# Routing's matmuls ahead of the linear layer's products within a step of TensorE

## The chip, the cores and the metric

The kernel runs on one core of a Trainium2 chip. A core has TensorE (matrix products, results in PSUM), VectorE, ScalarE and GpSimd, each with a list of its own that it works through in order, and SyncE, which starts DMAs. The lists are tied together by semaphores: an instruction waits until a count is reached. The metric is the time on the device in microseconds; lower is better.

## The reference, cut to what matters

Four layers over x, 2048 tokens of 512 floats (8 x 256 x 512), each with a layer norm ahead and x added behind. The change touches the first two.

```python
x = x + attn0(layernorm(x))     # data @ (blockwise masked weight).T + bias
x = x + ffn0(layernorm(x))      # routing, below
x = x + attn1(layernorm(x))     # latent K/V attention, 32 heads
x = x + ffn1(layernorm(x))      # gated feed forward, 1376 wide

# ffn0
logits = flat @ router_weight.T + router_bias       # 64 experts
scores = softmax(logits)
topk_w, topk_idx = top_k(scores, 8)
out = flat * topk_w.sum(-1) + w_dense @ expert_bias  # w_dense: topk_w at topk_idx
```

## The kernel before

The first stages run over 16 tiles of 128 tokens in a software pipeline. `head_steps` makes the steps s = 0 to 30; in step s the linear layer (`SparseLinear`) works on tiles near s and routing (`RoutedBias`) on tiles near i = s - 6. Each engine has its own loop over the steps and takes the linear layer's part, then routing's, then K/V tasks (`now`), which exist only from step 23 on. There is no planner; the order within a step is the order in the code.

TensorE's part of a step, with the letters used below (line numbers are those of the profile's rows):

- F, `flip`, L714: four transposes that turn linear's h of tile s - 2 into a bank of PSUM (steps up to 17).
- P, the products, L738: twelve matmuls of 512 columns for tile s - 3 (three passes over high and low parts, four chunks), in steps 3 to 18. P waits for the low part of the turned tile (`lo_done`) from VectorE, and gives `y_done`.
- C, L937: one transpose of the chosen experts' weights, tile i - 4, from step 10 on.
- N, L945: four transposes of the next layer's h, tile i - 9, from step 15 on.
- M, L952: the mix, one product with the experts' bias, tile i - 5, from step 11 on.
- L, L959: the logits, four small products, tile i - 2, from step 8 on.
- T, L967: four transposes of routing's h, tile i - 1, from step 7 on. T and C write the same bank of PSUM (`ps_c = ps_t`), so each waits until ScalarE has copied out the result of the other (`await_turn_bank`).

The order before is F, P, C, N, M, L, T. At i = 0, which is step 6, TensorE also waits for routing's constants (`await_constants`), behind F and P of that step. Their last writer is GpSimd, with two memsets (L825, L827) in its own step 6. GpSimd's part of step 6 waits for other tiles' results, not for P of step 6.

ScalarE's part of a step is: the high part of F's turned tile (L67, h_hi), linear's h of the next tile (L121), exp of the logits (L860), the scaling of x (L865, needs r_combined from GpSimd), the copy of C's result (L870, r_chosen_t), the high part of N's result, routing's h (L121), the copy of T's result (L885, h1t) and the high part of one piece of K/V weights (kv_w_hi).

VectorE's part begins with the addition of P's result of the step before to x (L695, waits for `y_done`), then the statistics of x for the next layer norm (L94, L98), the low part of the turned tile (L72), and routing's top 8 and additions. GpSimd's part begins with the bias addition (L632), then the layer norm's factors (L102, L106, L108; the first L102 waits for VectorE's statistics mv_ln), routing's next h (L116), r_combined (L849, L852) and the low part of a piece of K/V weights (L72, kv_w_lo, which waits for kv_w_hi).

In the texts P(6) is P of step 6, F(10) is F of step 10, and so on.

Of the kernel before, what the change touches and what calls it, by code (L numbers as in the profile page):

```python
# [530 lines left out]
class SparseLinear:  # L531
# [190 lines left out]
        pe.matmul(self.ps_b, self.same_block[:, :], self.row_sums[:, :], start=True, stop=True).then_inc(self.blocks_done, 1)  # L722
        self.flip(pe, 1)

    def pe_body(self, pe, i):
        if 2 <= i - 2 < TILES:
            self.flip(pe, i - 2)
        if 0 <= i - 3 < TILES:
            t = i - 3
            pe.wait_ge(self.lo_done, t + 1)  # L730
            if t >= 2:
                pe.wait_ge(self.x_done, t - 1)
            tokens = self.tokens(t)
            for c in range(KC):
                if t == 0:
                    pe.wait_ge(self.w_lo_done, c + 1)
                for n, (a, b) in enumerate(PASSES):
                    last = pe.matmul(self.ps_y[:, t % 2, :], tokens[a][:, c, :], self.w0[b][:, c, :],  # L738
                                     start=(c == 0 and n == 0), stop=(c == KC - 1 and n == 2))
            last.then_inc(self.y_done, 1)  # L740
# [257 lines left out]
def first_stages(nc, sem, sb, ps, split, x, ident, half, consts, ln, weights, h3, kv_w, query, operands, sources, router_sources, kv_weights, wq_g, k_scr, v_scr):  # L998
# [14 lines left out]
    with ExitStack() as st:  # L1013
# [8 lines left out]
        with ExitStack() as shared:  # L1022
            linear = SparseLinear(sem, sb, split, bank, x, ident, half, consts, ln[0], ln[1], h3, sources, shared)
# [19 lines left out]
        def freed(eng, n):  # L1043

            before = [m for m in range(n) if bank_of[m] == bank_of[n]]
            if not before:
                if bank_of[n] >= 4:
                    eng.wait_ge(routed.lo_done, TILES)
                else:
                    eng.wait_ge(linear.lo_done, TILES)  # L1050
                    eng.wait_ge(linear.x_done, TILES)
            elif before[-1] in down_count:
                eng.wait_ge(z_done, down_count[before[-1]])
            elif before[-1] in stage_count:
                eng.wait_ge(staged, stage_count[before[-1]] + 1)
            else:
                eng.wait_ge(lo_done, lo_count[before[-1]])

        def outlet(n):

            _, _, a, b = tasks[n]
            return ([p[:, a, :, 4 * b:4 * b + 4, :].rearrange("p b h m -> p h b m") for p in latent],
                    bank[:, bank_of[n], :].rearrange("p (h b m) -> p h b m", h=4, b=4))
# [28 lines left out]
        with nc.Block() as block:  # L1092
            @block.gpsimd
            def _(pool):
                linear.pool_start(pool)
                for s, i, p, _ in steps:
                    if s >= 2:
                        linear.pool_body(pool, s)
                    if i == 0:
                        routed.set_constants(pool, linear)  # L1100
                    routed.pool_body(pool, i)
                    if 0 <= p < KV_PIECES:
                        piece_lo_part(pool, p)
                query.make(pool, 0)
# [80 lines left out]
            @block.vector  # L1185
            def _(dve):
                def task(n):
                    if n in lo_count:
                        dve.wait_ge(hi_done, lo_count[n])
                        parts, src = outlet(n)  # L1190
                        lo_part(dve, parts, src).then_inc(lo_done, 1)
                    if n in given_at:
                        query.given_lo_part(dve, given_at[n], 0)
                    if n in step_lo_at:
                        operands.step_lo(dve, step_lo_at[n])
                    if n in step_at:
                        if step_at[n] == 0:
                            dve.wait_ge(routed.lo_done, TILES)
                            dve.wait_ge(piece_lo, KV_PIECES)
                        operands.step_sum(dve, step_at[n])  # L1200

                linear.dve_start(dve)
                for s, i, _, now in steps:
                    if s >= 2:
                        linear.dve_body(dve, s)
                    if i == 0:
                        routed.await_constants(dve)
                    routed.dve_body(dve, i)
                    for n in now:
                        task(n)  # L1210
                for n in range(paired, len(tasks)):
                    task(n)

            @block.tensor
            def _(pe):
                awaited = set()

                def task(n):
                    kind, quad, a, b = tasks[n]
                    if kind in pieces_of and kind not in awaited:  # L1220
                        awaited.add(kind)
                        pe.wait_ge(piece_lo, pieces_of[kind])
                    freed(pe, n)
                    out = bank[:, bank_of[n], :]
                    if kind == "Z":
                        pe.wait_ge(routed.lo_done, (quad + 1) * TILES // 2)
                        for c in range(KC):
                            for m, (u, v) in enumerate(PASSES):
                                tokens = h3[u][:, c, quad * SPAN:(quad + 1) * SPAN].rearrange("p (n j) -> p n j", j=8)[:, :, a]
                                last = pe.matmul(out, tokens, down_w[v][:, c, :], start=(c == 0 and m == 0), stop=(c == KC - 1 and m == 2))  # L1230
                    elif kind == "C":
                        pe.wait_ge(z_done, down_count[at[("Z", quad, 2 * a + 1, 0)]])
                        for h in range(4):
                            last = pe.transpose(out[:, h * P:(h + 1) * P], z[:, a % 2, 4 * b + h, :, :].rearrange("p j l -> p (j l)"), ident[:, :])
                    elif kind == "K":
                        if (a, b) == (0, 0):
                            pe.wait_ge(lo_done, lo_count[at[("C", quad, 1, 1)]])
                        for c in range(2):
                            for m, (u, v) in enumerate(PASSES):
                                last = pe.matmul(out, up_w[0][u][:, c, b * HEAD:(b + 1) * HEAD],  # L1240
                                                 latent[v][:, c, 2 * a:2 * a + 2, :, :].rearrange("p b h m -> p (b h m)"),
                                                 start=(c == 0 and m == 0), stop=(c == 1 and m == 2))
                    else:
                        if (a, b) == (0, 0):
                            pe.wait_ge(lo_done, lo_count[at[("C", quad, 3, 1)]])
                        for c in range(2):
                            for m, (u, v) in enumerate(PASSES):
                                rows = latent[u][:, 2 + c, a // 2, 4 * (a % 2):4 * (a % 2) + 4, :].rearrange("p h m -> p (h m)")
                                last = pe.matmul(out, rows, up_w[1][v][:, c, b * HID:(b + 1) * HID],
                                                 start=(c == 0 and m == 0), stop=(c == 1 and m == 2))  # L1250
                    last.then_inc(task_done, 1)

                linear.pe_start(pe)
                for s, i, _, now in steps:
                    if s >= 3:
                        linear.pe_body(pe, s)
                    if i == 0:
                        routed.await_constants(pe)
                        pe.wait_ge(linear.on_done, 1)
                    routed.pe_body(pe, i)  # L1260
                    for n in now:
                        task(n)
                for n in range(paired, len(tasks)):
                    task(n)
# [1155 lines left out]
```

## Time and profile before

| what | us |
|---|---|
| median of 3 runs | 1679.67 (1678.84 to 1681.83) |
| the profiled execution, its own time | 1679.91 |
| its span, first to last instruction | 1678.0 |
| TensorE busy | 1631.0 |
| VectorE, ScalarE, GpSimd busy | 1164.2, 924.4, 843.8 |
| mean granted clock of TensorE | 0.997 |

The span is the profile's own clock, from the first instruction to the last; the execution's time has 1.91 us more around it. Rows of a timeline give the start, the duration, the engine, the line of the kernel, the operation and the tiles out<-in; a bracket gives the engine's idle time just before and what released it. "L738" there is a line of the kernel, while L alone is the letter for the logits. Matmuls overlap, so the distance from one start to the next says how long one holds the engine, not its duration.

### The profile page before, as it was taken

To read this page: it belongs to the slowest core of one execution; us is meant where nothing else is said; L and a number is where in the kernel's file an instruction comes from. 1 tells how busy PE (TensorE), PEld (TensorE's weight loads), DVE (VectorE), ACT (ScalarE), POOL (GpSimd) and SP (SyncE) were. 2 spreads that over 40 slices of the span, in tenths; PEclk is the share of its full clock that TensorE was granted. 3 is DMA by queue.
4 is the path that set the end of the run, shared out by engine and by line. 5 is a ranking of instruction groups with operands and counts; after the bars stand their busy time and mean duration, and the time that the engine had idled before them with its cause. 6 is when DMAs were issued, how large, how long until landed. Compare 5 with 4: busy or idle time off the path is not lost. (4 is left out here: it accounts for less than half of the span.)

```text
span 1678.0 us, 26468 instructions
## 1 busy us (share of the span) xinstructions
PE 1631.0 (97%) x8298; PEld 1370.3 (82%) x8298; DVE 1164.2 (69%) x2990; ACT 924.4 (55%) x2464; POOL 843.8 (50%) x1257
## 2 busy tenths in 40 slices
PE   6989999999999999999999999999999899999999
PEld 4868887788888888888888888888888788877887
DVE  6883254776776776667667767767767588787776
ACT  3764455665765665666566556657657443434432
POOL 4883003634634644544445346446446297708752
PEclk9999999999999999999999999999999999999999
DMA  5011754111111111134111111111110021113111
GB/s 170 26 29 60 274 178 145 51 63 38 51 64 38 41 51 54 46 101 163 64 40 50 63 39 51 63 39 51 64 38 26 32 76 63 39 32 113 51 51 50
DMA packets 62489, 114.98 MB, mean 69 GB/s; under 512 B 5584, under 2 KB 25040, under 8 KB 58256
## 3 DMA queue, kind: packets, MB, share of 16 engines
q1 hardware_dynamic: 62352, 113.30, 20.4%
q8 instruction: 68, 1.11, 0.3%
q14 instruction: 69, 0.57, 0.1%
HBM read 84.97 MB, written 28.31 MB: 68 GB/s over the span
## 5 line engine op out<-in xcount | busy, mean ns | idle before, releaser
L1854 PE MATMUL ps_q<-kv_w_hi,o_hi 128*128 128x512 f32 x512 | 203.5, 397 | 4.5 <-DVE o_lo L72 4.5
L1854 PE MATMUL ps_q<-kv_w_lo,o_hi 128*128 128x512 f32 x512 | 200.0, 391 | 0.0
L1854 PE MATMUL ps_q<-kv_w_hi,o_lo 128*128 128x512 f32 x512 | 199.7, 390 | 0.0
L72 POOL TENSOR_TENSOR kv_w_lo<-w_raw,kv_w_hi 128x512 fp32r<-128x512 f32 x128 | 163.1, 1291 | 57.3 <-ACT kv_w_hi L67 57.3
L1796 PE MATMUL ps_q<-h_hi,kv_w_hi 128*128 128x512 f32 x448 | 181.9, 406 | 3.0 <-PEq L1092 1.5
L1796 PE MATMUL ps_q<-h_lo,kv_w_hi 128*128 128x512 f32 x448 | 175.4, 392 | 0.0
L1796 PE MATMUL ps_q<-h_hi,kv_w_lo 128*128 128x512 f32 x448 | 175.0, 391 | 0.0
L67 ACT ACTIVATE kv_w_hi<-w_raw 128x512 fp32r<-128x512 f32 (+1 forms) x240 | 126.6, 566 | 64.1 <-POOL w_raw L260 62.8
L1383 POOL TENSOR_SCALAR prob<-prob,inv_sum 128x128 f32<-128x128 f32 x256 | 95.3, 372 | 103.6 <-DVE inv_sum L1601 103.3
L67 ACT ACTIVATE o_hi<-ps_o 128x512 fp32r<-128x512 f32 x128 | 76.3, 596 | 127.2 <-PE ps_o L1836 127.1
L1439 ACT ACTIVATE prob<-prob,neg_max 128x128 f32<-128x128 f32 x256 | 100.2, 392 | 83.0 <-DVE neg_max L1596 83.0
L255 POOL TENSOR_TENSOR w_raw<-w_raw 128x512 f32<-128x512 f32 x16 | 26.4, 1648 | 220.1 <-DVE kv_w_lo L72 220.1
L1626 DVE TENSOR_TENSOR x<-ps_q,x 128x512 f32<-128x512 f32 x128 | 87.8, 686 | 67.7 <-PE ps_q L1854 67.7
L72 POOL TENSOR_TENSOR h_lo<-v_raw,h_hi 128x512 fp32r<-128x512 f32 x32 | 41.1, 1283 | 184.8 <-ACT h_hi L67 184.8
L1441 ACT ACTIVATE prob<-prob,neg_max 128x256 f32<-128x256 f32 x256 | 126.8, 495 | 0.0
L72 DVE TENSOR_TENSOR o_lo<-ps_o,o_hi 128x512 fp32r<-128x512 f32 x128 | 88.0, 688 | 51.3 <-ACT o_hi L67 51.2
L1384 POOL TENSOR_SCALAR prob<-prob,inv_sum 128x256 f32<-128x256 f32 x256 | 122.7, 479 | 0.0
L1594 DVE CUSTOM_DVE_ANT_0 prob<-ps_s,causal 128x128 f32<-128x128 f32 x256 | 74.3, 290 | 66.0 <-PE ps_s L1812 64.8
L1854 PEld LDWEIGHTS ps_q<-kv_w_hi,o_hi 128*128 128x128 f32 x512 | 96.2, 188 | 28.5 <-issue 10.4
L1854 PEld LDWEIGHTS ps_q<-kv_w_lo,o_hi 128*128 128x128 f32 x512 | 96.1, 188 | 20.5
L2329 PE MATMUL f_ps_r<-h_hi,kv_w_hi 128*128 128x512 f32 x280 | 109.5, 391 | 2.1 <-DVE f_part_U L2203 1.9
L1854 PEld LDWEIGHTS ps_q<-kv_w_hi,o_lo 128*128 128x128 f32 x512 | 96.3, 188 | 18.3
(236 smaller groups left out, 4868.1 us busy)
## 6 DMA issues: line engine op xcount, KB each, us to landing
w_raw<-in_wq_g SPq DMA_DIRECT2D x16, 1024.0 KB, 4.8
w_raw<-in_wo_g SPq DMA_DIRECT2D x16, 1024.0 KB, 4.7
k_raw<-k_scratch SPq DMA_DIRECT2D x32, 256.0 KB, 3.4
v_raw<-v_scratch SPq DMA_DIRECT2D x32, 256.0 KB, 3.8
f_gate_raw<-in_gate_c SPq DMA_DIRECT2D x10, 512.0 KB, 4.9
f_up_raw<-in_up_c SPq DMA_DIRECT2D x10, 512.0 KB, 3.6
f_down_raw<-in_down_c SPq DMA_DIRECT2D x10, 512.0 KB, 4.0
x<-in_x SPq DMA_DIRECT2D x16, 256.0 KB, 2.8
```

What stands on the lines that cost most here:

```text
L67: return act.activation(parts[HI], src, ACT.Copy)
L72: return dve.tensor_tensor(parts[LO], src, parts[HI].bitcast(F32), ALU.subtract)
L255: pool.tensor_tensor(self.block("S1"), self.block("A21"), self.block("A22"), ALU.add).then_inc(self.made, 1)
L1383: pool.tensor_scalar(prob[:, b, h, 0:P], prob[:, b, h, 0:P], inv_sum[:, b, h, 0:1], 1.0, ALU.mult, ALU.mult)
L1384: pool.tensor_scalar(prob[:, b, h, P:3 * P], prob[:, b, h, P:3 * P], inv_sum[:, b, h, 1:2], 1.0, ALU.mult, ALU.mult).then_inc(normed, 1)
L1439: act.activation(prob[:, b, h, 0:P], prob[:, b, h, 0:P], ACT.Exp, scale=-1.0, bias=neg_max[:, b, h, 0:1], accum_out=row_sum[:, b, h, 0:1])
L1441: act.activation(prob[:, b, h, P:3 * P], prob[:, b, h, P:3 * P], ACT.Exp, scale=-1.0, bias=neg_max[:, b, h, 1:2], accum_out=row_sum[:, b, ...
L1594: dve.tensor_tensor_reduce(out=prob[:, b, h, 0:P], in0=ps_s[:, h, 0:P], in1=causal[:, P:2 * P], scale=-SCALE, scalar=3.0e38, op0=ALU.add, ...
L1626: dve.tensor_tensor(x[:, t, :], ps_q[:, half, :], x[:, t, :], ALU.add).then_inc(y_read, 1)
L1796: done = pe.matmul(ps_q[:, i, :], left[s][:, c, i * HEAD:(i + 1) * HEAD], right[t][:, c, :], start=(c == 0 and m == 0), stop=(c == 1 and m ...
L1854: done = pe.matmul(ps_q[:, half, :], o[b][i][:, half, h, :], wo[j][:, h, :], start=(h == 0 and m == 0), stop=(h == GROUP - 1 and m == 2))
L2329: last = pe.matmul(bank(kind, k, name), stationary[a], feed.operand(right)[b][:, c, :], start=(c == 0 and m == 0), stop=(c == 1 and m == 2))
```

## The change

`pe_body` of the linear layer is cut in two: `pe_flips` holds F, `pe_products` holds P. TensorE's loop calls the first where `pe_body` was and the second behind routing's part. The order of a step becomes F, C, N, M, L, T, P, and in step 6 P also comes behind the wait for the constants. The other engines' lists, all instructions and all DMAs are the same.

```diff
-    def pe_body(self, pe, i):
+    def pe_flips(self, pe, i):
         if 2 <= i - 2 < TILES:
             self.flip(pe, i - 2)
+
+    def pe_products(self, pe, i):
         if 0 <= i - 3 < TILES:
             t = i - 3
             pe.wait_ge(self.lo_done, t + 1)
@@
                 for s, i, _, now in steps:
                     if s >= 3:
-                        linear.pe_body(pe, s)
+                        linear.pe_flips(pe, s)
                     if i == 0:
                         routed.await_constants(pe)
                         pe.wait_ge(linear.on_done, 1)
                     routed.pe_body(pe, i)
+                    if s >= 3:
+                        linear.pe_products(pe, s)
                     for n in now:
                         task(n)
```

## Rows read from the trace of the kernel before

**Rows 1.** The page: busy time of each engine over the span.
```profile
PE 1631.0 (97%) x8298; PEld 1370.3 (82%) x8298; DVE 1164.2 (69%) x2990; ACT 924.4 (55%) x2464; POOL 843.8 (50%) x1257
```

**Rows 2.** Windows: length; busy PE, PEld, DVE, ACT, POOL; granted clock; DMA share, GB/s.
```profile
34.40:37.80 3.40, 3.34 (x10) 2.86 (x11) 2.78 (x7) 2.00 (x3) 2.39 (x6) 0.52 0.00 0
...
106.00:109.50 3.50, 3.33 (x11) 2.33 (x11) 2.80 (x11) 2.07 (x8) 2.97 (x9) 0.53 0.02 5
...
121.50:185.00 63.50, 63.09 (x296) 56.18 (x296) 20.81 (x42) 29.44 (x59) 15.54 (x31) 1.00 0.27 97
```

**Rows 3.** Waits from 29 to 122 us: in total, times, longest.
```profile
ACT x L865 <- POOL r_combined L852: 12.4, 8, 2.7
...
PE kv_banks L937 <- ACT h1t L885: 4.7, 5, 1.0
...
POOL kv_w_lo L72 <- ACT kv_w_hi L67: 2.6, 2, 2.3
```

**Rows 4.** Timeline of TensorE, steps 6 to 18: start, duration, what.
```profile
28.86 0.60 PE L714 MATMUL kv_banks<-ident,h 128*128 128x128 f32 x4
...
34.46 1.11 PE L714 MATMUL kv_banks<-ident,h 128*128 128x128 f32 x4 [2.25 <-POOL r_chosen L827]
...
44.23 0.60 PE L714 MATMUL kv_banks<-ident,h 128*128 128x128 f32 x4
...
47.43 1.00 PE L959 MATMUL kv_banks<-router,h1t 128*128 128x64 f32 x8
...
52.02 1.00 PE L959 MATMUL kv_banks<-router,h1t 128*128 128x64 f32 x8
52.86 0.61 PE L967 MATMUL kv_banks<-ident,h 128*128 128x128 f32 x4
53.30 0.60 PE L714 MATMUL kv_banks<-ident,h 128*128 128x128 f32 x4
...
80.99 0.63 PE L967 MATMUL kv_banks<-ident,h 128*128 128x128 f32 x4 [0.30 <-ACT r_chosen_t L870]
...
94.17 0.48 PE L738 MATMUL kv_banks<-w_hi,h_hi 128*128 128x512 f32 x1
...
97.00 0.27 PE L937 MATMUL kv_banks<-ident,r_chosen 128*128 128x128 f32 x1
...
98.41 1.00 PE L959 MATMUL kv_banks<-router,h1t 128*128 128x64 f32 x8
```

**Rows 5.** Timeline of ScalarE, steps 6, 11 and 15.
```profile
29.50 0.60 ACT L67 ACTIVATE h_hi<-kv_banks 128x512 fp32r<-128x512 f32 x1 [1.90 <-PE kv_banks L714]
...
54.30 0.59 ACT L67 ACTIVATE h_hi<-kv_banks 128x512 fp32r<-128x512 f32 x1
54.78 0.81 ACT L121 ACTIVATE h<-x,factors_ln 128x512 f32<-128x512 f32 x1
55.48 0.34 ACT L860 ACTIVATE r_exp<-logits,r_neg_max 128x64 f32<-128x64 f32 x1
...
79.87 0.81 ACT L865 ACTIVATE x<-x,r_combined 128x512 f32<-128x512 f32 x1 [1.50 <-POOL r_combined L852]
80.59 0.26 ACT L870 ACTIVATE r_chosen_t<-kv_banks 128x128 f32<-128x128 f32 x1
```

**Rows 6.** Timeline of VectorE, steps 8, 14, 15 and 19; GpSimd's last.
```profile
39.51 0.69 DVE L695 TENSOR_TENSOR x<-kv_banks,x 128x512 f32<-128x512 f32 x1 [2.25 <-PE kv_banks L738]
...
70.25 0.68 DVE L695 TENSOR_TENSOR x<-kv_banks,x 128x512 f32<-128x512 f32 x1
...
75.97 0.68 DVE L695 TENSOR_TENSOR x<-kv_banks,x 128x512 f32<-128x512 f32 x1
...
100.90 0.68 DVE L695 TENSOR_TENSOR x<-kv_banks,x 128x512 f32<-128x512 f32 x1
...
102.28 0.18 DVE L98 BATCH_NORM_AGGREGATE mv_ln<-bn_ln 128x2 f32<-128x6 f32 x1
...
104.12 0.21 POOL L102 TENSOR_SCALAR ve_ln<-mv_ln 128x1 f32<-128x1 f32 x1
```

## The prediction

> **What bounds the kernel now.** I read the page first: TensorE is busy for 97% of the span [rows 1]. That is an average, so the second view is the windows over the stage that the change touches (steps 6 to 18 of the first stages, about 29 to 104 us). It shows where TensorE is not full: at 34.4 us it comes back from a wait at half clock (0.52), and at 106 us again (0.53); from 121.5 us on it is busy for 63.09 of 63.50 us [rows 2]. So two things count: when the first K/V product starts (121.5 us), because behind it TensorE alone sets the pace, and what sets that start.
>
> The list of waits for 29 to 122 us says what does: ScalarE waits 12.4 us in 8 places for GpSimd's r_combined [rows 3]. GpSimd is the slow engine of the steady state, and TensorE and ScalarE stand by for it. In TensorE's own timeline the steps 8 to 13 have no gap at all, and from step 15 on T waits for the copy of the turned choice (80.99, 0.30 idle) [rows 4]. GpSimd needs from TensorE, above all, the statistics of x behind each P: VectorE adds the product to x, takes the statistics, and GpSimd's first piece for that tile (L102) starts right behind them. At 39.51 VectorE itself waited 2.25 us for a P [rows 6]. Therefore the question is when the P of each step ends, up to the last one in step 18.
>
> **What the change moves.** No instruction is added or taken away, no DMA moves, and no queue but TensorE's changes. In each of the steps 6 to 18 the twelve matmuls of P go behind C, N, M, L and T. In steps 3 to 5 nothing of routing exists, so nothing moves. Three costs follow.
>
> *1. Step 6.* There is nothing of routing in it but the wait for the constants, and that wait now stands ahead of P(6), the products of tile 3, which used to run from 29.2 us. GpSimd's memset releases it at 34.46 us [rows 4], and its own work doesn't depend on P(6). So P(6) starts at 34.46. The engine then works at half clock, 0.52 for 3.40 us [rows 2], which costs 3.40 x 0.48 = 1.63 us against full clock. P alone is 97.00 - 94.17 = 2.83 us. P(6) ends at 34.46 + 2.83 + 1.63 = 38.9. Step 7 is then F and P (47.43 - 44.23 = 3.20) and T (0.44, from 52.86 to 53.30): F(8) at 42.6. Steps 8 and 9 are F and P, L (52.86 - 52.02 = 0.84) and T, 4.48 us each, as before: F(9) at 47.0, F(10) at 51.5, where it was at 44.23 + 4.48 = 48.7 [rows 4]. TensorE is 2.8 us late.
>
> *2. Steps 10 to 17.* From step 10 on T overwrites the bank of C, so it waits until ScalarE has copied C's result out. Before, P stood between F and T and hid that wait. Now F (0.37), C, N and M (1.41) and L (0.84) stand ahead of T, 2.6 us at most, and P stands behind T. ScalarE's list of the step starts with the copy of F's result, so each step is one closed chain: F start to copy 29.50 - 28.86 = 0.64; copy to h 0.48; h to exp 0.70; exp 0.34 [rows 4, 5]; scale to chosen copy 80.59 - 79.87 = 0.72 [rows 5]; that copy to T 80.99 - 80.59 = 0.40; T 0.44; P 2.83; and then the next F. Sum 6.55 us. Seven steps (10 to 16) give F(17) at 51.5 + 45.9 = 97.4, where TensorE's own work was only 4.6 to 5.9 us a step. In step 17 the h of linear's next tile is gone (0.70 less): 103.2. Step 18 has no F, and TensorE's work fills it: C, N, M 98.41 - 97.00 = 1.41, L 52.86 - 52.02 = 0.84, T 0.44, P 2.83 [rows 4], together 5.5: P(18) ends at 108.8. VectorE's add of it starts 0.2 later at 109.0, where it was at 100.90; its aggregate ends 102.28 + 0.18 - 100.90 = 1.56 us behind that and GpSimd's L102 follows, at 110.6, where it was at 104.12 [rows 6]. So GpSimd is 6.5 us late. In the list of waits GpSimd has only early ones [rows 3], so there is no idle time from here to step 22 to give back, and behind 121.5 us TensorE is full [rows 2], so 6.5 us reach the end. That the late start and the loop are not added in full (P(18) is 11.8 us late, GpSimd 6.5) is because VectorE used to take P(18) 3.9 us after its end.
>
> The sum hangs on 8 handoffs. The row has 80.99 - 80.85 = 0.14 us from the end of ScalarE's copy to T [rows 4, 5]. The Trainium skill (Runtime: NRT & Kernel Launch, the section on the preamble) gives 44 ns for a semaphore's hop between engines in a barrier; with that figure, as an estimate, 8 x 0.10 = 0.8 us less, so 5.7. No run here shows a barrier's hop in this place, and the sum keeps the trace's 0.14.
>
> *3. The clock.* In step 10 TensorE has F, C and L, about 1.3 us, but not yet N and M; T can start 0.64 + 0.48 + 0.70 + 0.34 + 0.72 + 0.40 = 3.28 us behind F, so it waits 2.0 us. The trace before has no such wait in this place. Nearest row: 2.25 us of idle before 34.46 and the clock is at half behind it [rows 2, 4]; from the other side: of five waits of up to 1.0 us for ScalarE's h1t, from 100 us on, one was followed by half clock, the others by full [rows 2, 3]. 2.0 us is nearest to the first. So I take one fall, for its price of 1.63 us; it lies on the closed chain (T and P of step 10) and goes to the end in full. The bounds are 0 and, with a second fall in a later step (each has 1.1 us of idle), 3.3.
>
> What costs nothing: C, N, M and L now run earlier, hidden under ScalarE's part of the chain; if ScalarE were quicker they would cost up to 2.6 us a step. VectorE's list of a step is 75.97 - 70.25 = 5.7 us long [rows 6], under the 6.55. In step 7 GpSimd's kv_w_lo waited 2.3 us for a copy behind T [rows 3]; T is now ahead of P(7), but P(6) is ahead of T, which starts at 38.9 + 0.4 = 39.3, so I book no gain (rival D has it).
>
> Sum: 6.5 + 1.6 = 8.1 us. The profiled execution's own time, 1679.91, gives 1688.0; it lies 0.24 above the median of the runs, 1679.67, which gives 1687.8 (+0.49%).
>
> **Rivals.**
> A, the clock stays up in step 10: for it, that 1.0 us waits mostly passed; against it, the length of the wait. 6.5 us, 1686.2. Chance 0.18.
> B, the clock falls again in steps 11 to 22: the waits of 1.1 us a step are new, and at 106 us it fell once in such a stretch, hidden by GpSimd then [rows 2, 3]. 8.1 + 1.6 to 3.3, about 1690.3. Chance 0.12.
> C, the other side, not slower: T's wait for ScalarE's copy stays covered, because the copy of F and the four activations get done while C, N, M and L run. Then a step lasts as long as TensorE's work (4.6 to 5.9 us), GpSimd sets the pace again from step 10, and at most the 2.8 us of point 1 are left: by a little less, 2.6 us, 1682.3, within the noise. It decides if ScalarE's part is under 2.6 us; the rows give 3.3. Chance 0.08.
> D, gain: the turn ahead of P gives ScalarE and GpSimd their work sooner, and GpSimd's 2.6 us of waits for kv_w_hi go [rows 3]. For it: GpSimd is the bound. It holds only if P(6) is done by the time VectorE was through with step 7, 39.51 - 2.25 = 37.3 [rows 6], against 38.9. 1677.1. Chance 0.05, half of it with more gain than the noise.
> My forecast has 0.57; its own range, with a chain of 6.3 to 6.8 us a step (0.25 either way, seven times), is 1686.5 to 1690.
>
> **How the numbers follow.** 0.2% is 3.4 us, about what a measurement of this kernel can tell from no change. Slower by more than that: forecast, A and B, 0.87. Within: C and half of D, 0.10. Faster: 0.03. The range has to take in A and the lower part of B, and reach towards C: 1683.5 to 1691.0 leaves out D, most of C and the upper part of B, under 2 in 10.
>
> **What the new profile would show.** TensorE idle about 5 us up to 34.46, then twelve L738-type matmuls first; VectorE's add of step 7 at 39.0 instead of 34.44. In each of the steps 10 to 17 T (the turn) with idle before it, released by ScalarE's r_chosen_t, 2.0 us in step 10 and 1.1 us after; F to F 6.55 us. A window of half clock from about 55 us. The last P ending near 110 us, GpSimd's waits for mv_ln appearing in steps 11 to 13 and 19, and the first K/V product at 128 to 130 us; everything behind it shifted and otherwise the same. The prediction is wrong if F to F stays at 5.5 us (C), if no window but 34.4 and one late one is at half clock (A), or if the K/V tasks win back time behind 130 us.

## The result, and the profile after

| | before | after |
|---|---|---|
| median (lowest to highest, runs) | 1679.95 (1678.84 to 1681.83, 4) | 1690.38 (1689.56 to 1693.94, 4) |
| profiled execution, its own time | 1679.91 | 1689.57 |
| its span | 1678.0 | 1687.6 |
| TensorE busy, mean granted clock | 1631.0, 0.997 | 1635.0, 0.994 |

The ratio is 1.0063 with an interval of [1.0052, 1.0075]: the change costs 0.63%, 10.5 us (8.7 to 12.6). The forecast was 1687.8, 8.1 us more; the range, 1683.5 to 1691.0, holds the median. One execution in this study, among the 12 of e7 below, took 2340.83 us at a mean granted clock of 0.655, and the comparisons leave it out. The kernel with the change has other line numbers: F is L714, P L740, C L939, N L947, M L954, L L961, T L969, GpSimd's last memset L829, ScalarE's copy of C L872, its copy of T L887.

The page's row of busy time. Against [rows 1] the averages say next to nothing: the same instructions, TensorE 4 us busier.

```profile
PE 1635.0 (97%) x8298; PEld 1374.3 (81%) x8298; DVE 1164.1 (69%) x2990; ACT 925.0 (55%) x2464; POOL 843.9 (50%) x1257
```

The waits from 29 to 135 us (total, times, longest) say where it went.

```profile
ACT h_hi L67 <- PE kv_banks L714: 28.4, 11, 9.1
DVE x L695 <- PE kv_banks L740: 19.4, 12, 8.2
POOL ve_ln L102 <- DVE mv_ln L98: 12.0, 7, 6.5
...
PE kv_banks L969 <- ACT r_chosen_t L872: 6.1, 7, 1.7
...
PE kv_banks L740 <- POOL r_chosen L829: 5.0, 1, 5.0
...
POOL kv_w_lo L72 <- ACT kv_w_hi L67: 0.8, 3, 0.3
```

In [rows 3] GpSimd was the engine that the others waited for: ScalarE stood by for r_combined, 12.4 us. That row is gone. Now GpSimd itself waits, 12.0 us (6.5 of them in step 7), for statistics that VectorE takes behind P, VectorE waits 19.4 us for P, ScalarE 28.4 us for F, and TensorE 6.1 us for ScalarE's copy of C. Each engine waits for the next one in a ring. GpSimd's wait for kv_w_hi fell from 2.6 to 0.8 us, but an engine that waits 12 us elsewhere gains nothing from that.

TensorE's timeline of step 6 and the start of step 7 (start, duration; a bracket is idle time before and what released it), to be read against [rows 4]:

```profile
27.28 0.60 PE L714 MATMUL kv_banks<-ident,h 128*128 128x128 f32 x4
32.84 0.80 PE L740 MATMUL kv_banks<-w_hi,h_hi 128*128 128x512 f32 x1 [4.96 <-POOL r_chosen L829]
...
38.12 1.02 PE L714 MATMUL kv_banks<-ident,h 128*128 128x128 f32 x4
```

And of steps 10 and 11, where T now stands ahead of P:

```profile
51.13 0.60 PE L714 MATMUL kv_banks<-ident,h 128*128 128x128 f32 x4
51.56 0.27 PE L939 MATMUL kv_banks<-ident,r_chosen 128*128 128x128 f32 x1
51.67 1.00 PE L961 MATMUL kv_banks<-router,h1t 128*128 128x64 f32 x8
54.40 0.63 PE L969 MATMUL kv_banks<-ident,h 128*128 128x128 f32 x4 [1.73 <-ACT r_chosen_t L872]
54.78 0.48 PE L740 MATMUL kv_banks<-w_hi,h_hi 128*128 128x512 f32 x1
...
57.63 0.60 PE L714 MATMUL kv_banks<-ident,h 128*128 128x128 f32 x4
...
60.90 0.63 PE L969 MATMUL kv_banks<-ident,h 128*128 128x128 f32 x4 [0.87 <-ACT r_chosen_t L872]
...
64.11 0.60 PE L714 MATMUL kv_banks<-ident,h 128*128 128x128 f32 x4
```

F to F is 6.50 and 6.48 us, with TensorE idle before each T. ScalarE's timeline of step 10 shows what T waits for: five activations back to back behind F, and the copy of C is the fifth.

```profile
51.76 0.60 ACT L67 ACTIVATE h_hi<-kv_banks 128x512 fp32r<-128x512 f32 x1 [1.34 <-PE kv_banks L714]
52.26 0.80 ACT L121 ACTIVATE h<-x,factors_ln 128x512 f32<-128x512 f32 x1
52.96 0.34 ACT L862 ACTIVATE r_exp<-logits,r_neg_max 128x64 f32<-128x64 f32 x1
...
53.29 0.81 ACT L867 ACTIVATE x<-x,r_combined 128x512 f32<-128x512 f32 x1
54.00 0.26 ACT L872 ACTIVATE r_chosen_t<-kv_banks 128x128 f32<-128x128 f32 x1
```

The windows (length; busy PE, PEld, DVE, ACT, POOL; granted clock; DMA share, GB/s) for the stretches behind a wait, for the start of K/V, and for three stretches far behind it:

```profile
32.80:38.60 5.80, 5.76 (x15) 4.51 (x16) 0.07 (x1) 0.00 (x0) 1.27 (x1) 0.50 0.00 0
51.10:57.60 6.50, 4.77 (x30) 4.11 (x29) 3.87 (x15) 4.10 (x9) 5.95 (x13) 1.00 0.06 20
113.00:119.00 6.00, 4.57 (x20) 3.35 (x20) 4.92 (x17) 3.42 (x9) 4.95 (x14) 0.72 0.10 27
128.40:192.00 63.60, 63.19 (x298) 56.24 (x298) 20.84 (x42) 29.50 (x59) 15.56 (x31) 1.00 0.26 97
285.00:315.00 30.00, 27.28 (x143) 22.78 (x141) 21.25 (x68) 19.95 (x62) 14.01 (x22) 0.94 0.25 81
1305.00:1335.00 30.00, 25.48 (x123) 20.40 (x122) 19.59 (x37) 9.81 (x18) 2.59 (x2) 0.94 0.11 35
1515.00:1545.00 30.00, 28.92 (x128) 24.01 (x129) 20.35 (x30) 13.84 (x31) 20.73 (x28) 0.94 0.42 140
```

The same three late stretches of the kernel before:

```profile
285.00:315.00 30.00, 26.95 (x146) 21.90 (x144) 23.69 (x71) 21.01 (x63) 15.07 (x23) 1.00 0.26 88
1305.00:1335.00 30.00, 26.96 (x138) 21.82 (x137) 17.88 (x34) 12.20 (x22) 4.11 (x5) 1.00 0.13 45
1515.00:1545.00 30.00, 28.70 (x125) 22.85 (x124) 20.91 (x29) 14.45 (x34) 25.98 (x32) 1.00 0.36 123
```

**Reading times from a common start.** The release, the end of GpSimd's last memset in step 6, fell at 34.41 us in the profile before and at 32.78 in the one after. The change doesn't set it. The kernel before had one more fall of the clock, from 20 to 24 us (the windows of before and after, in this order):

```profile
20.00:24.00 4.00, 3.15 (x10) 2.67 (x11) 2.11 (x5) 2.09 (x3) 3.44 (x5) 0.61 0.64 182
20.00:24.00 4.00, 3.18 (x16) 2.71 (x17) 2.09 (x5) 2.11 (x3) 3.80 (x6) 1.00 0.55 190
```

GpSimd's L102 of step 5, which waits for VectorE's statistics, then started at 27.93 us for 26.32. In eleven of the fourteen profiles of this study the release lies between 32.78 and 32.95; e11, at 34.52, has the same early fall (0.62), and e1 is at 33.35 without it. So stages are compared in time behind the release. "Tail" is the span behind the first K/V product.

| us behind the release | before | after | later by |
|---|---|---|---|
| F(10) | 14.30 | 18.35 | 4.05 |
| F(17) | 53.91 | 63.77 | 9.86 |
| VectorE's add of P(18) | 66.49 | 75.63 | 9.14 |
| GpSimd's first L102 of step 19, the one in [rows 6] | 69.71 | 77.30 | 7.6 |
| first K/V product | 87.12 | 95.69 | 8.57 |
| tail | 1556.5 | 1559.1 | 2.7 |

The span grew by 9.6 us: the release came 1.6 earlier, the stage up to K/V took 8.57 more, the tail 2.7 more. The tail has the same work (63.19 of 63.60 us busy here, 63.09 of 63.50 in [rows 2]), but the granted clock is 0.94 in three stretches of 30 us where it was 1.00. That is 0.06 x 30 = 1.8 us of lost clock each, not all of it on the path.

### The profile page after: what moved, and what is told of

Same layout as the page of the kernel before. It is cut to its first block and busy times, and to the rows that moved or that the text cites. A ratio compares the mean times of both kernels' runs of the same rounds, so it can differ in the third digit from the quotient of the medians.

```text
span 1687.6 us, 26468 instructions
## 1 busy us (share of the span) xinstructions
PE 1635.0 (97%) x8298; PEld 1374.3 (81%) x8298; DVE 1164.1 (69%) x2990; ACT 925.0 (55%) x2464; POOL 843.9 (50%) x1257
## 5 line engine op out<-in xcount | busy, mean ns | idle before, releaser
L255 POOL TENSOR_TENSOR w_raw<-w_raw 128x512 f32<-128x512 f32 x16 | 26.4, 1648 | 219.4 <-DVE kv_w_lo L72 219.4
L2333 PE MATMUL f_ps_r<-h_hi,kv_w_hi 128*128 128x512 f32 x280 | 109.5, 391 | 2.0 <-DVE f_part_U L2207 1.8
```

Of the source, the lines that this page charges most:

```text
L2333: last = pe.matmul(bank(kind, k, name), stationary[a], feed.operand(right)[b][:, c, :], start=(c == 0 and m == 0), stop=(c == 1 and m == 2))
```

## The experiments

Each of the twelve is compared with runs of the kernel before on the same chip. The medians of the kernel before range from 1679.95 to 1681.23 us over the chips, so an expected time can be off by about 1 us for that alone. The columns: ratio to before with its interval; then, from one profile each, the time from release to F(10) and to the first K/V product, and the tail.

| kernel | ratio | F(10) | K/V | tail |
|---|---|---|---|---|
| before | 1 | 14.30 | 87.12 | 1556.5 |
| after | 1.0063 [1.0052, 1.0075] | 18.35 | 95.69 | 1559.1 |
| a2_again | 1.0055 [1.0042, 1.0068] | 17.36 | 97.60 | 1558.2 |
| e1_p6_first | 1.0031 [1.0018, 1.0043] | 14.27 | 93.18 | 1559.3 |
| e2_only_step6 | 1.0021 [1.0012, 1.0029] | 17.74 | 91.19 | 1559.5 |
| e3_t_last | 1.0036 [1.0024, 1.0048] | 19.28 | 94.27 | 1558.3 |
| e7_warm | 1.0032 [1.0022, 1.0042] | 15.94 | 93.92 | 1558.7 |
| e5_act_order | 1.0033 [1.0020, 1.0046] | 17.24 | 91.23 | 1561.7 |
| e6_shift | 1.0039 [1.0025, 1.0053] | 14.28 | 87.14 | 1566.6 |
| e8_variance | 0.9984 [0.9975, 0.9994] | 12.67 | 82.19 | 1558.7 |
| e11_late_wait | 0.9986 [0.9977, 0.9995] | 10.26 | 83.51 | 1558.1 |
| e12_late_var | 0.9955 [0.9943, 0.9968] | 10.23 | 80.78 | 1558.7 |
| e14_after_both | 0.9997 [0.9988, 1.0006] | 10.22 | 87.22 | 1561.3 |
| e15_all | 0.9986 [0.9977, 0.9995] | 10.20 | 87.04 | 1557.9 |

**The two parts of the change, apart.** In e1 P(6) runs ahead of the wait for the constants, as before, and the other steps are as changed. In e2 only P(6) is moved behind the wait.

```diff
# e1_p6_first
                     if i == 0:
+                        linear.pe_products(pe, s)
                         routed.await_constants(pe)
...
-                    if s >= 3:
+                    if s >= 3 and i != 0:
                         linear.pe_products(pe, s)
# e2_only_step6
                         linear.pe_flips(pe, s)
+                    if s >= 3 and i != 0:
+                        linear.pe_products(pe, s)
                     if i == 0:
                         routed.await_constants(pe)
                         pe.wait_ge(linear.on_done, 1)
+                        linear.pe_products(pe, s)
                     routed.pe_body(pe, i)
-                    if s >= 3:
-                        linear.pe_products(pe, s)
```

> The change in all steps but step 6, where P(6) stays ahead of the wait for the constants. Theory (two costs: the wait in step 6, and the closed chain through T in steps 10 to 17): in the changed kernel's trace F(10) is 4.0 us late against the release of the constants, so that part goes and the chain stays, F to F 6.5 us in steps 10 to 16, and P(18) ends some 8 us later than before; GpSimd's first piece of step 19 is late by 3.6 us instead of 7.6. Time 4.0 us under the changed kernel, about 1686 (1684 to 1687). Rival, the step 6 wait is nearly all of it: 1680 to 1682. Rival, the chain is all of it: 1690.

> The order of before in all steps but step 6, where P(6) stands behind the wait for the constants. Theory: F(10) 4 us late, then TensorE's own work (4.6 to 5.9 us a step) runs without the chain and GpSimd, which is slower from step 12 on, hides part of it: 3 us over before, about 1683 (1681.5 to 1684.5). Rival, the step 6 wait is nearly all of the loss: 1688 to 1690. Rival, GpSimd hides all of it: 1680.

e1 cost 5.2 us (3.0 to 7.2), e2 3.5 us (2.0 to 4.9); their medians, 1687.25 and 1684.84, lie 0.3 us over the upper ends of the expected ranges. Their sum, 8.7, is near the change's 10.5 and a2's 9.2, so both parts are real and add up. K/V says the same: it is 6.06 us late in e1 and 4.07 in e2, and e1's profile has a fall of the clock in step 10, worth 1.6 us (below), that after's hasn't; 6.06 + 4.07 - 1.6 = 8.5 for 8.57. In e1 F(10) is where it was before (14.27), and from there every step is the closed chain. In e2 F(10) is 3.44 us late, the add of P(18) 3.39 (69.88 for 66.49) and K/V 4.07: F to F is 5.44 to 5.45 in steps 11 to 14, as before, and nothing of the late start is won back on the way, where I had expected GpSimd to hide part of it. (The 0.7 us from 3.39 to 4.07 come with a fall of the clock, 0.51 from 112.8 to 116.2 us.)

**T behind P.** F, C, N, M, L, P, T: if only T's wait ahead of P costs, moving T back should leave little more than e2.

```diff
                     if s >= 3:
                         linear.pe_products(pe, s)
+                    routed.pe_turn(pe, i)      # T, cut out of routed.pe_body
```

> The changed kernel with T behind P instead of ahead of it: F, C, N, M, L, P, T. P(6) still stands behind the wait for the constants. Theory: the chain F, ScalarE's copies, T, P is open again, since P no longer waits for ScalarE; F to F is TensorE's own 4.6 to 5.9 us in steps 10 to 14, and what is left is step 6's part: 3 to 4 us over before, about 1683.5 (1682 to 1685). Rival, it is not T's wait but P's late place in the step (VectorE's add comes late) that costs: 1688 to 1690.

It cost 6.0 us (1687.34 for the expected 1682 to 1685), and so the expectation failed. TensorE's timeline of steps 13 and 14 of e3 (P's rows left out, which run from 72.32 to 75.19):

```profile
69.51 0.60 PE L714 MATMUL kv_banks<-ident,h 128*128 128x128 f32 x4
70.45 0.30 PE L939 MATMUL kv_banks<-ident,r_chosen 128*128 128x128 f32 x1 [0.34 <-ACT h1t L887]
...
75.19 0.60 PE L971 MATMUL kv_banks<-ident,h 128*128 128x128 f32 x4
75.62 0.60 PE L714 MATMUL kv_banks<-ident,h 128*128 128x128 f32 x4
```

T no longer waits, but the bank is shared both ways: only F is left between T and the next C, where the order before has F and P, and C waits for ScalarE's copy of T. F to F is 6.11 us, and P still ends late in the step. How much of the 6.0 us is that late place and how much the wait, e3 alone doesn't tell; e14 below has P late without the closed chain and stands level with before.

**ScalarE's list.** If F to F is a chain through ScalarE, then taking F's copy and linear's h from ahead of the exp, the scaling and the copy of C should cut it, with TensorE's order as changed.

```diff
                 for s, i, p, now in steps:
+                    routed.act_chosen(act, i)   # L862, L867, L872, cut out of routed.act_body
                     if s >= 3:
                         linear.act_body(act, s)
```

> The changed kernel's TensorE order, with ScalarE's exp, scaling of x and copy of C taken ahead of linear's copy of F and h in each step. Nothing else differs. Theory: the chain of steps 10 to 17 is F, ScalarE's copy of F, h, exp, scaling, copy of C, T, P, F; with F's copy behind the copy of C it is cut, T waits no more and F to F is TensorE's own 5.45 us in steps 11 to 14. What is left is step 6 and the late P: 1684 to 1686, 4 to 6 us under the changed kernel. Rival, another wait takes its place (T or C for h1t, as with T behind P): F to F about 6 us, 1687. Rival, T's wait was not the cost: 1690.

TensorE's timeline of one step of e5:

```profile
60.85 0.60 PE L714 MATMUL kv_banks<-ident,h 128*128 128x128 f32 x4
...
63.09 0.61 PE L971 MATMUL kv_banks<-ident,h 128*128 128x128 f32 x4
...
66.29 0.60 PE L714 MATMUL kv_banks<-ident,h 128*128 128x128 f32 x4
```

T has no idle time before it, and F to F is 5.44 us in steps 11 to 13, TensorE's own work, where it was 6.50. For these steps that shows that the loop was this chain. In steps 14 to 16 F to F is 6.66 to 6.85 us: T waits again (1.01 and 0.78 us in steps 14 and 15), with ScalarE waiting for VectorE's r_neg_max and GpSimd's r_combined. The order before isn't at 5.45 there either (6.36 and 6.87 in steps 15 and 16), and over all of F(10) to F(17) the chain's loss is in steps 10 to 14: 32.5 us in after for 26.4 in before, and 13.0 for 13.2 in the two steps behind.

K/V comes 4.5 us sooner than in after (91.23 for 95.69). 1.1 us of that lies ahead of F(10), and 0.9 is the fall of the clock at 114 us that after has and e5 hasn't (see "From 6.5 to 8.57"). From F(10) to K/V before takes 72.8 us, e5 74.0 and after, less that fall, 76.4, so e5 takes away two thirds of what the chain costs there. By the ratios e5 is 5.5 us over before, where the change is 10.5, or 9.2 on e5's own chip (a2); e5's tail is 2.6 us longer than after's.

**Is the price of step 6 the clock?** e7 is the changed kernel with 52 small transposes into an unused bank ahead of the wait, so that TensorE is not idle in it.

```diff
                     if i == 0:
+                        for _ in range(52):
+                            pe.transpose(bank[:, 7, 0:P], ident[:, :], ident[:, :])
                         routed.await_constants(pe)
```

> The changed kernel with 52 extra transposes of the identity into an unused bank between F(6) and the wait for the constants, so that TensorE isn't idle there (they are no part of the computation). Theory: the half clock from 32.8 to about 38.6 us in the changed kernel's trace comes from that idle time and costs 5.8 x 0.5 = 2.9 us on the chain; it goes: 1687.5 (1686.5 to 1688.5), with F(10) about 2.9 us earlier against the release. Rival, the half clock comes anyway or GpSimd hides it: 1690 or above.

Windows of e7: behind the release, and step 10.

```profile
32.90:36.00 3.10, 3.10 (x18) 2.64 (x17) 0.00 (x0) 0.00 (x0) 1.28 (x1) 1.00 0.00 0
48.80:57.00 8.20, 6.47 (x32) 5.38 (x31) 3.84 (x15) 4.10 (x9) 7.01 (x14) 0.79 0.11 32
```

The clock is at 1.00 where it was at 0.50. From the start of P(6) to F(8) e7 takes 6.47 us and after 9.36, so the half clock costs 2.89 us. F(10) comes only 2.4 us sooner behind the release, since the transposes ran past it: P(6) starts 0.52 us behind the release in e7 and 0.06 in after. The second window shows the clock falling in step 10, which after's own profile doesn't have (1.00 from 51.1 to 57.6), so part went back. In sum e7 cost 5.4 us over before.

**The change once more,** for the clock in step 10:

> The changed kernel once more, for a second profile and a comparison of its own on the chip of the next three. Theory: the stretch from the release of the constants to the first K/V product is 95.7 us again (87.1 before), while the falls of the clock lie elsewhere from profile to profile: 1687 to 1692, and a fall in step 10 (F to F 8.1 us instead of 6.5) is seen in some profiles, as in the two experiments before, and not in others.

TensorE's timeline of step 10 and the window over it, in a2:

```profile
50.21 0.60 PE L714 MATMUL kv_banks<-ident,h 128*128 128x128 f32 x4
...
53.48 0.63 PE L969 MATMUL kv_banks<-ident,h 128*128 128x128 f32 x4 [1.73 <-ACT r_chosen_t L872]
...
54.26 0.63 PE L740 MATMUL kv_banks<-w_hi,h_lo 128*128 128x512 f32 x1
...
58.30 0.60 PE L714 MATMUL kv_banks<-ident,h 128*128 128x128 f32 x4
```

```profile
50.20:58.30 8.10, 6.37 (x31) 5.25 (x30) 3.84 (x15) 4.10 (x9) 7.03 (x15) 0.79 0.12 32
```

Same kernel, same wait of 1.73 us, and now the clock falls behind it: products of 0.63 us for 0.39, F to F 8.09 for 6.50, so 1.6 us. Of the five profiles with a wait of 1.73 us or more in step 10 four have the fall (a2, e1, e7, e14), after has not. In e5 the wait is 0.53 us and the clock stays up.

Of the expectation the clock came true and the stretch did not: K/V stands at 97.60 us and not at 95.7. F(10) is 1.0 us sooner than in after, step 10 takes 1.6 us more, and behind P(18) a2 is at half clock for twice as long as after, 21.36 us from the add of P(18) to K/V for 20.06:

```profile
115.50:122.40 6.90, 6.12 (x23) 4.40 (x21) 4.50 (x21) 4.77 (x12) 5.68 (x13) 0.51 0.15 39
```

**Does a shift ahead of K/V reach the end?** e6 is the kernel before, with 70 transposes behind the first K/V task.

```diff
                     for n in now:
                         task(n)
+                        if n == 0:
+                            for _ in range(70):
+                                pe.transpose(bank[:, 3, 0:P], ident[:, :], ident[:, :])
```

> The kernel before, with 70 extra transposes of the identity into an unused bank behind the first K/V product group (they are no part of the computation), some 6.5 to 7.5 us of TensorE time. Theory: from the first K/V product TensorE alone sets the pace, so the whole of it reaches the end: 1687 to 1688, plus 0 to 3 us where the clock falls lie otherwise than in the kernel before. Rival, later stages have slack that takes it up: under 1684.

The filler's row in e6's timeline:

```profile
123.11 7.80 PE L1265 MATMUL kv_banks<-ident 128*128 128x128 f32 x70
```

7.8 us put in, 6.5 us (4.2 to 8.9) at the end, 8.6 us in the profiled span. Within the interval all of it arrives. Up to K/V e6 is the kernel before a second time: 87.14 us for 87.12. And yet before has the fall at 106 us [rows 2] and e6 is at 1.00 from 104 to 112 us: in the order before, where GpSimd is the late engine, that fall costs nothing.

**Toward a better kernel.** Two ideas from the same reading, on the order before. e8 takes L102 from GpSimd, the engine that sets the pace, to VectorE, in both layer norms that stand there: from step 12 on that is two instructions a step. e11 takes TensorE's and VectorE's wait for the constants from step 6 to step 8, where the first logits need them. e12 has both.

```diff
# e8_variance: out of GpSimd's loop, into VectorE's; linear's part, then routing's
-            self.ln_next.variance(pool, i - 5)
+            self.ln_next.variance(dve, i - 5)
...
-            self.ln_next.variance(pool, t)
+            self.ln_next.variance(dve, t)
# e11_late_wait: in VectorE's loop, and in TensorE's
-                    if i == 0:
+                    if i == 2:
                         routed.await_constants(dve)
...
                     if i == 0:
-                        routed.await_constants(pe)
                         pe.wait_ge(linear.on_done, 1)
+                    if i == 2:
+                        routed.await_constants(pe)
```

> The kernel before with the epsilon addition of the two next layer norms (L102) on VectorE instead of GpSimd. Theory: GpSimd bounds steps 12 to 20 of the kernel before; it gives up 0.31 us in 12 steps and another 0.31 in 8, and VectorE has 0.2 us for each: the first K/V product comes 3 to 5 us earlier against the release (82 to 84 us instead of 87.1), 1675 to 1678. Rival, TensorE's and VectorE's own lists (5.45 to 5.9 us a step) take over at once: 1679 to 1680.

> The kernel before with the wait for routing's constants moved from step 6 to step 8 on TensorE and VectorE, where the first routing instruction that needs them or the weights stands. Theory: in step 6 TensorE and VectorE wait 2.3 and 2.5 us for GpSimd's memsets with work ready; F(7), P(7) and T(7) then start at about 32 instead of 34.5, without the fall of the clock (1.6 us), and GpSimd's wait of 2.3 us for kv_w_hi in step 7 goes: the first K/V product 2 to 3 us earlier, 1677 to 1678.5. Rival, GpSimd bounds from step 9 on whatever starts earlier: 1680.

> The late wait and the epsilon additions on VectorE together, in the order before. Theory: both take work or waits from GpSimd and add up where it is the bound: 2.7 us from the second as measured, 2 from the first: 1674.5 to 1676. Rival, TensorE's own list takes over as the bound and the first adds nothing: 1677.

e8 brings K/V 4.9 us forward and the time down by 2.7 us (1.0 to 4.2). In GpSimd's timeline of after one such instruction holds the engine for 0.29 us, start to start:

```profile
104.39 0.21 POOL L102 TENSOR_SCALAR ve_ln<-mv_ln 128x1 f32<-128x1 f32 x1 [0.52 <-DVE mv_ln L98]
104.68 0.57 POOL L106 TENSOR_TENSOR factors_ln<-ve_ln,bn_ln 128x1 f32<-128x1 f32 x1
```

Not all of the 4.9 us is GpSimd's. e8's profile has the same wait of 2.25 us ahead of F(7) as before, and no half clock behind it:

```profile
32.91 0.66 PE L715 MATMUL kv_banks<-ident,h 128*128 128x128 f32 x4 [2.25 <-POOL r_chosen L828]
33.00:36.00 3.00, 3.00 (x16) 2.54 (x17) 2.73 (x8) 2.00 (x3) 1.67 (x2) 1.00 0.03 5
```

So F(10) is 1.6 us sooner by the clock, and the instructions have 3.3 us at K/V. e12 against e11, with the same F(10), gives 2.7 us for them.

e11 takes away the 2.25 us of idle and the half clock behind it [rows 2, 4]: F(10) is 4.04 us sooner, K/V 3.6, the time 2.4 us less (0.8 to 3.9). e12, 1673.62 us in five runs, is the best of all, 7.6 us (5.4 to 9.6) under before and better than the 1674.5 to 1676 that I expected; K/V is 6.3 us sooner. The change did the opposite with the same wait: it put more work behind it, e11 less.

**Does the change pay once its costs are cured?** e14 is the changed order with e11's late wait and e5's ScalarE order. e15 is e12 with e5's ScalarE order.

> The changed kernel's TensorE order with both costs taken away: the wait for the constants in step 8 (TensorE and VectorE) and ScalarE's exp, scaling and copy of C ahead of F's copy. Theory (these two are the whole loss): the time of the kernel before or a little under, 1679 to 1681, with F to F 5.45 us in steps 11 to 14. Rival, P's late place in the step costs by itself (VectorE's add and GpSimd's factors later by the 2.6 us of C, N, M, L and T): 1682 to 1684.

> The order before with the late wait, the epsilon additions on VectorE and ScalarE's routing part ahead of F's copy. Theory: in the order before no chain runs through T and P, so ScalarE's order adds nothing over the late wait and the additions alone: 1674.5 to 1676.5. Rival, it gives GpSimd and TensorE their inputs sooner in steps 19 to 23: 1 to 2 us less. Rival, F's high part comes later and holds up P: 1 to 3 us more.

e14 is where before is (0.9997), so the two cures pay for all of the loss, and the rival, that P's late place costs 1 to 3 us by itself, doesn't show. It isn't a gain: e11 with the order before has 0.9986, though the two intervals overlap, and its K/V 3.7 us sooner. e14's profile has the clock fall of step 10 too, behind a wait of 1.91 us. e15 is 5.2 us over e12 (1678.80 for 1673.62), K/V 6.3 us later, against the 1674.5 to 1676.5 that I expected. Waits of e15 from 45 to 114 us:

```profile
ACT r_exp L860 <- DVE r_neg_max L929: 15.0, 9, 2.3
...
PEld kv_banks L715 <- ACT h L121: 2.3, 5, 0.7
```

With the exp first in ScalarE's list, the whole list stands behind VectorE's maximum, F's copy and linear's h among it, and TensorE then waits for that h. F to F is 6.47 us in steps 14 to 16 of e15; in e12 it is 5.44, 5.89 and 5.86. Of the 6.3 us 4.9 are there by the add of P(18). e5's order opened one chain and made another; with T ahead of P it was still the better one.

## Why the forecast held, and where it was short

**Step 6.** Right in mechanism. TensorE was idle 4.96 us up to the release and began with P; VectorE's add of step 7 waited 8.2 us. Its size was short: I took the half clock as 3.40 us long, from [rows 2], for 1.63 us; in after, where the engine had been idle for 4.96 us and not 2.25, the clock was at 0.50 from 32.2 to 39.0 us, and that cost 2.89 us. F(10) was 4.05 us late for 2.8. In a2 it was 3.06 and in e2 3.44, so 1.2 us is the most that this term was off in these three. e2 alone shows the part at 3.5 us of the whole.

**The closed chain.** Right. Forecast 6.55 us F to F, measured 6.49 ((63.77 - 18.35) / 7); T's idle time 1.73 us in step 10, 0.87 in steps 11 to 14, 0.43 in 15 and 16 and none in 17, for 2.0 and 1.1 throughout; F(17) to VectorE's add of P(18) 11.86 for 11.6. GpSimd's waits for mv_ln in steps 11 to 13 and 19 stand where the forecast had them, with one more in step 18. e5 takes the chain apart and gets 5.44 in steps 11 to 13. The hop that the sum hung on was 54.26 to 54.40, 0.14 us, as in the rows. The Trainium skill's 44 ns (Runtime: NRT & Kernel Launch, the section on the preamble), which is given for a barrier, would have made seven steps 0.7 us too short, by the same estimate as in the prediction; the measurement decides for 0.14 here.

**From 6.5 to 8.57.** GpSimd's L102 of step 19 was 7.6 us late for the forecast's 6.5, and the difference is the half clock of step 6. (The prediction calls this L102 the first piece for P(18)'s tile. It works on the tile before, and stands behind P(18) only by VectorE's list. That P(18) was to be 11.8 us late and GpSimd 6.5 is the 3.9 us that the prediction names and 1.66 us that GpSimd's L102 used to come behind its input, at 104.12 for 102.46, less the 0.2 us to the add.) Behind it stands what I hadn't seen at all: from there to K/V after took 1.0 us more than before. At 113 to 119 us the clock is 0.72 in after. Before, the fall at 106 us [rows 2] was hidden by GpSimd, as e6 shows; now GpSimd is waiting there too (1.06 us, for mv_ln), and TensorE had C and N waiting for VectorE's r_chosen and h_lo, 1.1 us each in the list of waits. Four profiles have the same order there and differ by the clock. e7 stayed at 1.00 and took 19.12 us from the add of P(18) to K/V; its window:

```profile
111.00:117.00 6.00, 3.40 (x20) 2.36 (x20) 5.69 (x20) 3.69 (x9) 5.21 (x13) 1.00 0.08 25
```

After and e1 (0.57 from 112 to 116 us) took 20.06 and 20.07, and a2, with the longer fall, 21.36. So the fall costs 0.9 us, and twice as long a one 2.2. No kernel of the study takes it away on purpose.

**The clock in step 10.** The forecast had one fall there for 1.63 us at 0.57, and none (rival A) at 0.18. The first profile was A's, with its mark, 1.00 in that window, so by the prediction's own sign the term of 1.63 us was wrong for it. a2, e1, e7 and e14 have the fall, at 1.6 us. So it is a matter of the execution and not of the kernel: with a wait of 1.73 us both happen. Rival A's case and the forecast's are both seen. Of rival B's falls there is none in steps 11 to 18 of after, with waits of T of 0.87 us and less, but there is the one at 113 us, in a2 too: both profiles of the change are a mixture of the cases that I had kept apart. The measured 1690.38 us lies on rival B's 1690.3, and that number proves nothing for B.

**Where luck helped.** The forecast had 8.1 us, and after's profile shows 8.57 at K/V, but not from the same terms: the 1.6 us of step 10 is absent, and 1.2 us more in step 6 and 0.9 us behind P(18), neither of them booked, stand in its place. In a2 step 10's 1.6 us is there, step 6's excess is 0.3 us and the fall behind P(18) costs 2.2, and K/V is 10.5 us late. The size of the chain was foreseen; that the sum came so near in the first profile was luck.

**The other rivals.** C, that T's wait stays covered, asked for F to F near 5.5 us: it is 6.5. D, the gain, asked for P(6) done before 37.3 us, which is 2.9 us behind the release: F(7) followed it 5.3 us behind the release (38.12 us in after), and GpSimd waited 12 us for what comes behind P. The forecast's 38.9 was 4.4 us behind the release; the half clock makes the difference.

**The tail.** I had "everything behind it shifted and otherwise the same". The shift arrives (e6), and for 158 us behind the first K/V product TensorE's rows in before and after stand within 0.1 us of each other. But the tail of before's profile, 1556.5 us, is the shortest of the fourteen; eleven others lie between 1557.9 and 1559.5 (e6 less its filler), e5 and e14 at 1561.7 and 1561.3. What differs are falls of the clock to half, 1.8 us of lost clock each: none in before, three between 285 and 1545 us in after, and four in e5 and e14, which add 0.91 from 260 to 280 us to the same three. The other ten profiles have one or two. So the longest tails have the most falls and the shortest has none. Two profiles can differ by 2 to 3 us in the tail, at the extremes of these fourteen by 5, either way. What makes them come or stay away wasn't settled: no run here varies it by itself.

## What to carry to other kernels

- A wait stands for its engine's whole list. Before work is moved behind a wait, ask who else waits for that work: here P(6) moved by 5 us behind a release that had nothing to do with it, and VectorE and GpSimd were idle with it. e11, the opposite move of the same wait, gained 2.4 us.
- Two engines that work off fixed lists and feed each other make a chain. In cyclic order this change only swapped F and P, and that was enough: F is what ScalarE's list starts with, and P between F and C was the time in which ScalarE worked it off. Add up one turn of such a chain (here F, ScalarE's list up to the copy that frees the bank, T, P) and compare it with the busiest engine's work for a step. Moving the copy ahead in ScalarE's list cured most of it in the changed order (e5) and made a new wait, for VectorE's maximum, in the order before (e15).
- Where TensorE looks full, the gain lay with the engine that sets the pace of the stage: two 128x1 instructions a step taken off GpSimd brought 2.7 us, and together with the cure of a wait that stood two steps too early 7.6.
- One profile's stage time holds the clock falls of that execution. Before a gain at a stage is put down to an edit, compare the granted clock there: of e8's 4.9 us 1.6 were a fall that didn't come.

## What the runs showed of the hardware

- The same kernel with the same 1.73 us of idle time on TensorE came back once at full clock (after) and once at half (a2). Over all kernels waits of 1.73 to 1.91 us in step 10 were followed by half clock in four profiles and by full in one. The Trainium skill (TensorE: Matmul & The Clock Gate, part 1) says that one kernel can spend a different number of matmuls at the low clock from run to run; after and a2 agree with it, and so do before and e6, the same instructions up to K/V: before is at 0.61 from 20 to 24 us and 0.53 from 106 to 109.5, e6 at 1.00 in both places.
- Behind 2.25 us of idle time ahead of F(7) the clock was at 0.52 for 3.40 us in before [rows 2, 4] and at 1.00 in e8. Behind 4.96 us it was at 0.50 up to 39.0 us in after, 2.9 us lost; in a2, also behind 4.96, a mean of 0.67 from 33 to 39 us is 2.0 us lost.
- Up to the first K/V product two executions of the same instructions agree to 0.02 us from the release on (before and e6), while the release differs by 1.6 us between these two, with the fall at 20 us, and the tail by 2.4 (e6 less its filler). So one span against another tells a change of 10 us here, but not one of 2; times from a common event tell hundredths, as long as no fall of the clock on the path differs (after and a2 are 1.9 us apart at K/V).
